# Masking the decays on GpSimd, loading the weights in three groups, and a new order of the steps

## What is computed

```python
q, k = silu(conv(xn @ Wq)), silu(conv(xn @ Wk))       # 12 heads of 64, conv has 4 taps
v    = silu(conv(xn @ Wv))                            # 12 heads of 128
gk   = -exp(A_log) * softplus(xn @ Wgk + dt_bias)
beta = sigmoid(xn @ Wb + b_b)
for t in range(L):                                    # per head
    S     = S * exp(g[t])
    delta = (v[t] - k[t] @ S) * beta[t]
    S     = S + outer(k[t], delta)
    o[t]  = q[t] @ S
attn = (rmsnorm(o) * gnorm * silu(xn @ Wg)) @ Wo
h    = silu(fq(xn) @ fq(w_gate).T) * (fq(xn) @ fq(w_up).T)
out  = x + attn + fq(h) @ fq(w_down).T
```

## Time and profile before

| what | us |
|---|---|
| median of 3 runs | 3115.01 |
| lowest and highest run | 3111.84, 3118.43 |
| profiled execution, its own time | 3109.63 |
| its span, first to last instruction | 3107.9 |
| mean granted PE clock, share of 2.4 GHz | 0.931 |

### The profile page before, as it was taken

One profiled execution on the slowest core, in us unless ns is written; L12 is line 12 of the kernel. 1 busy time (PEld: TensorE's weight loads), 2 busy tenths in 40 slices (PEclk: granted clock), 3 DMA queues, 4 the chain that ended last, 5 costly groups with the idle time before them and its releaser, 6 DMA issues. The chain is left out here.

```text
span 3107.9 us, 84227 instructions
## 1 busy us (share of the span) xinstructions
PE 2683.1 (86%) x25361; PEld 2160.6 (70%) x25487; DVE 2498.6 (80%) x7140; ACT 2210.9 (71%) x6626; POOL 1621.8 (52%) x2418
## 2 busy tenths in 40 slices
...
GB/s 52 32 32 15 33 34 32 28 36 16 31 36 27 34 32 17 33 35 26 35 24 24 35 26 35 36 14 33 36 25 36 25 24 34 35 26 35 25 22 22
DMA packets 319515, 92.14 MB, mean 30 GB/s; under 512 B 283056, under 2 KB 310000, under 8 KB 318960
## 3 DMA queue, kind: packets, MB, share of 16 engines
...
## 5 line engine op out<-in xcount | busy, mean ns | idle before, releaser
L611 POOL TENSOR_TENSOR laneA<-laneA,laneT 96x30 f32<-96x30 f32 (+14 forms) x960 | 518.8, 540 | 75.2
L608 POOL TENSOR_TENSOR laneT<-laneA 96x30 f32<-96x30 f32 (+14 forms) x960 | 494.5, 515 | 70.4
L911 DVE SCALAR_TENSOR_TENSOR vc<-ring,cvv,vc 128x255 f32<-128x255 f32 (+2 forms) x1152 | 463.8, 472 | 22.3 <-ACT vc L713 22.0
L911 DVE SCALAR_TENSOR_TENSOR KQ<-ring,ckq,KQ 128x255 f32<-128x255 f32 (+2 forms) x1152 | 460.0, 472 | 16.5 <-DVE nabs L943 6.5
L622 POOL TENSOR_TENSOR rO<-ov,mhalf 128x8 f32<-128x8 f32 x96 | 159.6, 1662 | 377.3 <-DVE ov L1060 371.7
L1004 DVE SCALAR_TENSOR_TENSOR UP<-ring,cj,gm 128x256 f32<-128x256 f32 x768 | 315.4, 475 | 44.6 <-PE ring L1190 39.0
L595 POOL TENSOR_TENSOR sqk<-sse,phalf 128x8 f32<-128x8 f32 x96 | 157.1, 1636 | 350.5 <-DVE sse L978 350.5
L808 ACT ACTIVATE junk<-V 128x128 f32<-128x128 f32 x768 | 230.3, 305 | 77.7 <-DVE V L1055 64.7
L1190 PE MATMUL ring<-KQ 64*128 64x256 f32 x768 | 238.2, 453 | 54.8 <-DVE KQ L911 41.3
L773 ACT ACTIVATE eps<-bank_e 128x128 f32<-128x128 f32 x384 | 105.8, 276 | 225.8 <-PE bank_e L1326 184.6
L589 POOL TENSOR_TENSOR gm<-g,mle 128x512 f32<-128x512 f32 x192 | 197.7, 1048 | 128.6 <-DVE UP L1004 72.4
...
## 6 DMA issues: line engine op xcount, KB each, us to landing
to_lanes<-UP SPq DMA_DIRECT2D x128, 96.0 KB, 2.8
...
UP<-from_lanes SPq DMA_DIRECT2D x128, 96.0 KB, 3.1
...
```

The costliest lines, as they stand in the source:

```text
L608: link(nc.gpsimd.tensor_tensor(t, A[:, 0:m, j:j + 1].broadcast_to([LANES, m, n]), A[:, j:j + 1, j + 1:BLK].broadcast_to([LANES, m, n]), AL ...
L611: link(nc.gpsimd.tensor_tensor(w, w, t, ALU.add))
L911: ins = nc.vector.scalar_tensor_tensor(acc[:, n, s:T], src[:, n * T:n * T + T - s], wt(n)[:, TAPS - 1 - s:TAPS - s], acc[:, n, s:T], ALU.m ...
```

## The change

The bf16 product of DD is gone. Instead a new step DDm multiplies the exponentials on POOL with the 0/1 mask mle, in place, and GRr waits for it (semaphore s_mask) and not for ACT. The loads are in three groups, each with its own semaphore: x of the first item and nine loads that the first projections and gates need; the value weights (two); and the late ones (eight: feed-forward, gnorm, Wo, Wg). The rounding and turning of the feed-forward weights, and wo times gnorm, move to FU 0 of the first item. LN's load of item 0 is now issued at the very start.

ORDER is new. The parts of it that are spoken of below, as they stand before and after:

- XN, XNr: first in the list for the next item; now near the end of the list before it (offset 2 in place of 1, XNr with a wait for GP 5, whose input buffer it overwrites). VT 3, VTr 3 go from the end of the list to its beginning (of the next iteration). VPs 4, VPs 5 and XR now stand at the end, where they stood behind the beginning or in the middle.
- Beginning of the list now: VT 3, ZB, QK 0, ZBr, QKr 0, VTr 3, VT 2, QK 1, QK 2, ZBe, QKt 0, ZBg, QK 3. The end: ... WO 4, WO 5, HTr 0, KTr 1, HT 1, VPs 5, LANEP 7, HTr 1, YOr.
- LN: from between VPt 0 and DD 3 to behind GRr 11.
- GRr: before, GRr 0 to 3, SE 3 to 5, GRr 4, SO 5, SE 6, GRr 5, XQ0's second half, SO 6, MX 2, SO 7, ..., GR 3, GRr 6, ... GRr 11 behind SE 9. Now GRr 0 to 3, QN 2, QN 3, DDg 5, SSr 1, all of XQ0, CJ 1, DDm 2, MX 1, DDm 3, SE 3, GRr 4, DDm 4, SE 4, GRr 5, DDm 5, QN 5, SSr 2, GR 3, GR 4, GRr 6, GRr 7, GR 5, CJ 2, GRr 8, GRr 9, SE 5, SO 5, GRr 10, GRr 11, MX 2, SE 6.
- DDm 0 stands behind VPt 2, DDm 1 behind MYr 0, both ahead of MZ 0.
- LOUT behind SE 7 (before, behind FUm 0 and ahead of SE 10); LANEP 0 and 1 ahead of OS 0, LANEP 2 and 3 behind OS 0 and OS 1, 4 to 7 behind OS 2 (before, all behind OS 0).

The diff, cut to its core:

```diff
-WEIGHTS_FROM, WEIGHTS_TO = ("ZBr", 0), ("QKt", 2)
+WEIGHTS_AT = ("FU", 0)
+NW_FIRST, NW_LATE = 9, 8
...
@@ block.sync: x, then Wk, Wq, Wgk, Wb, conv_k, conv_q, dt_bias, b_b, A_log @@
+                sp.dma_start(xin[:, :, :], x_v[0]).then_inc(s_x, 16)
                 sp.dma_start(wqk[:, 0, :], Wk).then_inc(s_wload, 16)
...
+                sp.dma_start(wv[:, :], Wv).then_inc(s_wval, 16)
+                sp.dma_start(cvv[:, :, :], conv_v.rearrange("(h c) t -> c h t", c=P)).then_inc(s_wval, 16)
...
+                sp.dma_start(wg[:, :], Wg).then_inc(s_wlate, 16)
...
@@ block.gpsimd @@
+                    if kind == "DDm":
+
+                        pool.wait_ge(read("DD", a), rv(i, "DD", a))
+                        nc.gpsimd.tensor_tensor(out=decay(a), in0=decay(a),
+                                                in1=mle[:, :].unsqueeze(1).unsqueeze(1).broadcast_to([P, 2, NT, P]),
+                                                op=ALU.mult).then_inc(s_mask, 1)
@@ block.scalar, XN (VP of the first item: wait for s_wval) @@
+                        if not early(i):
+
+                            split(act, full("XN", 0), full("GP", 5))
+                            act.wait_ge(full("GP", 5), rv(i - 2, "GP", 5))
@@ block.vector @@
-            dve.wait_ge(s_wload, 16 * 19)
             dve.wait_ge(s_setp, 3)
...
             def feed_forward_weights(link):
 
+                dve.wait_ge(s_wlate, 16 * NW_LATE)
+                nc.vector.tensor_scalar(wo[:, :, :], wo[:, :, :], gw[:, 0:1], None, ALU.mult).then_inc(s_setd, 1)
...
-                    if zero(i) and (kind, a) == WEIGHTS_FROM:
+                    if zero(i) and (kind, a) == WEIGHTS_AT:
                         feed_forward_weights(link)
-                    if zero(i) and (kind, a) == WEIGHTS_TO:
                         turned_weights(link)
...
-                        dve.wait_ge(read("DD", p), rv(i, "DD", p))
+                        dve.wait_ge(s_mask, cnt(i, NP, p + 1))
@@ block.tensor @@
-            pe.wait_ge(s_setd, 1)
+            pe.wait_ge(s_wload, 16 * NW_FIRST)
...
-                        mm(b[:, :], mgt[:, :], decay(a).rearrange("p h t n -> p (h t n)"), start=True, stop=False)
-                        mm(b[:, :], identb[:, :], negm[:, :, :].rearrange("p u n -> p (u n)"), start=False, stop=True)\
+                        mm(b[:, :], mgt[:, :], decay(a).rearrange("p h t n -> p (h t n)"), start=True, stop=True)\
                             .then_inc(full("DD", a), 1)
```

More of the change, by code:

```diff
@@ L26 @@
 KEEP = ((("ZBr", 0, 1), ("XQ0", 0, 1)), (("ZB", 0, 1), ("QK", 2, 1)), (("ZBr", 0, 1), ("QKt", 2, 1)), (("QK", 2, 1), ("FU", 0, 1)), (("GPr", 0, 0), ("OG", 0, 0)), (("GPr", 1, 0), ("OG", 1, 0)), (("GPr", 2, 0), ("OG", 2, 0)), (("GPr", 3, 0), ("OG", 3, 0)), (("GPr", 4, 0), ("OG", 4, 0)), (("GPr", 5, 0), ("OG", 5, 0)))
-WEIGHTS_FROM, WEIGHTS_TO = ("ZBr", 0), ("QKt", 2)
+WEIGHTS_AT = ("FU", 0)
+NW_FIRST, NW_LATE = 9, 8
 ORDER = (
[L53 to L66, removed]
[7 rows of a table removed]
-    ("XQr", 0, 1), ("SQ", 9, 0), ("GRr", 9, 1), ("SE", 9, 0), ("GRr", 10, 1), ("GRr", 11, 1), ("SO", 9, 0),
[8 rows of a table removed]
-    ("GP", 2, 0), ("OTr", 0, 0), ("GPr", 2, 0), ("KTr", 1, 1), ("OTr", 1, 0), ("SO", 16, 0), ("SE", 16, 0),
[5 rows of a table removed]
-    ("OG", 4, 0), ("OT", 4, 0), ("GPr", 5, 0), ("VTr", 3, 1), ("OTr", 3, 0), ("LANEP", 6, 1), ("HT", 0, 1),
-    ("OG", 5, 0), ("WO", 3, 0), ("OTr", 4, 0), ("OT", 5, 0), ("HT", 1, 1), ("OTr", 5, 0), ("WO", 4, 0),
-    ("WO", 5, 0), ("HTr", 0, 1), ("LANEP", 7, 1), ("HTr", 1, 1), ("VPt", 5, 1), ("YOr", 0, 0),
@@ new lines @@
+    ("VT", 3, 0), ("ZB", 0, 1), ("QK", 0, 1), ("ZBr", 0, 1), ("QKr", 0, 1), ("VTr", 3, 0), ("VT", 2, 0),
+    ("QK", 1, 1), ("QK", 2, 1), ("ZBe", 0, 1), ("QKt", 0, 1), ("ZBg", 0, 1), ("QK", 3, 1), ("QKr", 1, 1),
+    ("QKt", 1, 1), ("VP", 0, 1), ("GC", 0, 1), ("DDg", 0, 1), ("VT", 5, 0), ("STORE", 0, 0), ("QKr", 2, 1),
+    ("QKt", 2, 1), ("QKr", 3, 1), ("VPr", 0, 1), ("TSTORE", 0, 0), ("VTr", 2, 0), ("TFETCH", 0, 0),
+    ("GCr", 0, 1), ("VTr", 5, 0), ("QKt", 3, 1), ("VP", 1, 1), ("QKs", 0, 1), ("QKs", 1, 1), ("QKs", 2, 1),
@@ new lines @@
+    ("VPr", 1, 1), ("VT", 4, 0), ("QK", 4, 1), ("DD", 0, 1), ("VTr", 4, 0), ("VPt", 1, 1), ("DDg", 1, 1),
+    ("DD", 1, 1), ("VP", 2, 1), ("QT", 0, 1), ("QKs", 3, 1), ("QKr", 4, 1), ("DDg", 2, 1), ("DDr", 0, 1),
+    ("QKt", 4, 1), ("VPr", 2, 1), ("FETCH", 0, 0), ("DD", 2, 1), ("DDr", 1, 1), ("QT", 1, 1), ("DDr", 2, 1),
+    ("QTr", 0, 1), ("VPt", 2, 1), ("DDm", 0, 1), ("MY", 0, 0), ("MY", 1, 0), ("MYr", 0, 0), ("DDm", 1, 1),
+    ("QT", 2, 1), ("QTr", 1, 1), ("QTr", 2, 1), ("QT", 3, 1), ("DDg", 3, 1), ("MZ", 0, 0), ("QN", 0, 1),
@@ new lines @@
+    ("QN", 1, 1), ("VPt", 0, 1), ("QK", 5, 1), ("MZr", 0, 0), ("MYr", 1, 0), ("DD", 3, 1), ("SSr", 0, 1),
+    ("MY2", 0, 0), ("QKr", 5, 1), ("DDr", 3, 1), ("QTr", 3, 1), ("CJ", 0, 1), ("MY2r", 0, 0), ("QKs", 4, 1),
+    ("QKt", 5, 1), ("GR", 0, 1), ("GRr", 0, 1), ("GRr", 1, 1), ("GR", 1, 1), ("QKs", 5, 1), ("GRr", 2, 1),
[4 rows of a table added]
+    ("DDm", 4, 1), ("SE", 4, 0), ("DDr", 5, 1), ("QTr", 5, 1), ("MZ", 2, 0), ("GRr", 5, 1), ("DDm", 5, 1),
+    ("QN", 5, 1), ("SSr", 2, 1), ("MZr", 2, 0), ("GR", 3, 1), ("GR", 4, 1), ("VPs", 0, 1), ("GRr", 6, 1),
[3 rows of a table added]
```

55 lines of the change are left out of this document (34 added, 21 removed), and 37 rows, old and new, of the table ORDER.

## The result

| | runs, us | profiled execution, us |
|---|---|---|
| kernel before | 3117.64 (3111.84 to 3123.48, 5 runs) | 3109.63 |
| changed kernel | 3095.24 (3092.36 to 3100.74, 5 runs) | 3095.24 |

The ratio is 0.9932, 95% interval 0.9914 to 0.995: faster by 0.7%. The forecast was 3092. The number came out 3 us off, but three of its terms were far off, and they cancelled. The page first: the busy line, then three of its groups (line, engine, operation, count, busy us, mean ns of one, idle time before it and what ended it).

A forecast was written before the change was run, and what follows sets the result against it. No engine bounds it everywhere: DVE the first stage, PE the last, the middle shared. 3109.6 - 19.5 (start) - 6 (turns) + 3 (iterations) = 3087, so 3092 for the runs' median; range 3045 to 3150.

The forecast's parts named there:

- The stages and the walk: One iteration: SO 5 comes later, PE's work and waits behind it shrink; +0.1 us with contention, bounds -1.5 and +2.5.
- rival A: PE's last stage: its waits go too, 1.5 us an iteration less, 3045; chance 0.12.
- Contention: XQ0 and CJ 1 on DVE beside POOL's DDg and DDm: one more wait, 0.6 us an iteration, at most 2.5.
- DDm 2 hidden with 2 us to spare: POOL ahead of GRr 4: some 4.2 us to DDm 2's end, covered by over 6 us of DVE work.
- The removed product: DD's bf16 product on PE: removal worth 0 to 1.3 us an iteration, nothing booked for it separately.
- The turns: 12 loop turns: with XN done before the turn, 0.5 us less each, 6 in all.
- The 5.5 stays: Loop turns: PE's 5.5 us idle while the branch is taken and code comes was to remain.
- The start: First iteration: split loads and postponed weights bring the next iteration 10.3 us earlier and remove a 9.2 wait, 19.5 together.
- no 9 us gap ahead of DD 0: After the first iteration: PE's 9.17 us wait for DDg behind the lane solve goes, since the solve ends early enough.
- rival D: Start: quantising the weights isn't hidden, 3103; chance 0.08.
- B: SO 5 too late: PE runs dry for GRr 4 to 9, perhaps half clock; +1.7 us an iteration, 3140; chance 0.35.
- C: POOL late: lane solve ends 1 us after PE asks for DD 0, each iteration 1 us longer, 3122; chance 0.05.

The follow-up runs named there:

- e1: Changed kernel with the mask back on PE (bf16 product in DD, no DDm on POOL), new order and weight groups kept: 2983.29 us, ratio to before 0.9581.
- e8: Changed kernel with both halves of XQ0 moved to the end of the iteration before, behind YOr, mask still on POOL: 3076.31 us.
- e12: As e9, but DDm 4 waits for GRr 4 on DVE and not for XQ0's end: 2982.39 us, ratio to before 0.9584.
- e3: Changed kernel with both halves of XQ0 moved in the order to behind GRr 11, nothing else: 3093.63 us.
- e9: Changed kernel with DDm 2 to 5 spread away from XQ0, DDm 4 and 5 waiting for XQ0's end: 3008.26 us.
- e5: Kernel before with the mask alone changed (DDm on POOL, DD one product), old order and old start: 3084.83 us.
- e2: Changed kernel with DDm cut from 512 columns to 16, order, waits and weight groups kept: 2972.39 us.
- e10: Kernel before with six more PSUM-clearing products at the start, 12 PE instructions ahead of the loop: 3057.87 us.
- e6: Kernel before with XN and XNr alone moved into the iteration before: 3055.59 us.
- e4: Changed kernel with the old start (one group of 19 loads, feed-forward weights quantised ahead of the first ZBr): 3109.71 us.

## Why the prediction was right in its number, point by point

- **The stages and the walk.** I forecast SO 5 4.6 us later in the iteration and the stretch behind it 5.1 shorter (3.5 of PE's work and 1.6 of waits), -0.5 together without contention. With SO 5 from its first instruction and the iteration from the end of YOr's copy, e1 has it 5.5 later and the rest 6.5 shorter (39.9 and 49.8 us before, 45.4 and 43.3 in e1). The walk was right to 1 us. By mean periods it is -1.55 a plain iteration. Small as that looks, the difference to my -0.5 stands for 30 iterations, 31 us of the sum, and it is the size that rival A gave to the last stage's waits.
- **Contention, the term that failed.** I took 0.6 us an iteration, one more wait of the kind of L839, with 2.5 as the upper bound, since POOL would also wait for CJ's power between DDm. It did so only once, between DDg 5 and DDm 2: DDr 2 to 5 came in time, so DDm 2 to 5 ran back to back and met four instructions of XQ0. That is 3.8 us of DVE and 3.6 of the period, beyond my bound, and 112 us in all (e1, e8, e12). I had counted conflicts, and should have laid POOL's queue beside DVE's.
- **The size of a DDm.** I used DDg's 1.05 for it. Undisturbed (e3, e9) it is 1.27, and 1.34 beside XQ0. Its first input is read in full where DDg's repeats one value, and it writes in place; which of the two makes the difference no run separates. That is +42 us of POOL on top of 201, hidden in itself, but it lengthens each conflict.
- **The rule of the Trainium skill** (SBUF — State Buffer, "Who interferes with whom") that I weighed as a danger held in the rows shown here. DVE instructions with two SBUF inputs, and a tensor_scalar of f32, wait for a whole POOL instruction (1.25 to 1.38); the taps (0.47), GRr (0.87 a pair), which have one input in PSUM, and the tensor_reduce of QN (0.68) keep their time. (One exception the other way: in e5 a tensor_scalar of two columns, `veps<-mv`, met DDm 13 times and kept its 0.17.) It did not hold for POOL's power: the product of L860, two SBUF inputs, began in its midst and took 0.42. There the measurement decides. I had the rule and the list of candidates, and booked one sixth.
- **DDm 2 hidden with 2 us to spare.** It was, behind XQ0; e3, which takes XQ0 away, shows the price without that cover: 2.35 us.
- **The removed product.** DD to DD is now 0.86 (two of them take 1.88, the last of which 1.02), as forecast. With the mask nearly free (e2 against e1) it is worth 0.3 us an iteration, from a range of 0 to 1.3.
- **The turns, the second failed term.** "The 5.5 stays", and 6 us for XN. It fell to 2.4 (29.2 us over 12, by PE's waits), and turns gained 5.4 each over plain iterations, 65 us in all. Measured in the same way, as what a turn adds to a plain period (8.45 before, 4.73 in e10, 3.53 in e6, 3.06 now), a shift of the code is worth 45 us (before to e10), XN's move another 14 (e10 to e6), and 6 are not separated. I took a wait named "issue" for one wait; it was two.
- **The start.** 19.5 forecast; in e4 18.7 at the first copy, and 14.5 to 18 in the time. From the kernel before to the changed one the first copy gains only 9.0, as with the old start (e4) the changed kernel reaches it 9.6 later than the kernel before: 6.6 of that is contention in the first two iterations (e1), the rest isn't separated. The steps:

```profile
13.99 2.43 DVE L926 SCALAR_TENSOR_TENSOR KQ<-ring,ckq,KQ 128x255 f32<-128x255 f32 x6 [1.43 <-ACT KQ L707]
...
61.10 2.12 SPq L497 DMA_DIRECT2D to_lanes<-UP  x4
...
64.71 1.01 DVE L879 TENSOR_SCALAR wo<-wo,gw 128x1536 f32<-128x1536 f32 x1
...
84.81 0.28 DVE L899 COPY wd<-bank_e 96x128 f32<-96x128 f32 x1
...
108.40 1.92 POOL L628 COPY laneX<-laneA 72x1024 f32<-72x1024 f32 x1 [0.18 <-POOL laneA L622]
108.91 0.21 DVE L958 TENSOR_TENSOR z<-ring,zbias 128x48 f32<-128x48 f32 x1 [1.42 <-PE ring L1169]
```

Taps at 14.0 for 15, LOUT at 61.1 for 60, the solve's end at 108.4 for 104, no 9 us gap ahead of DD 0 (in e4 it is 10.22). But the next iteration's ZBr stood at 108.9: the weights took DVE 20.4 us with the waits for their transposition, not 16.4, and the work behind them 23.8, not 18. In e4 this ZBr stands at 116.25, so the new start is worth 7.3 us there, where I had 10.3; the 3 missing are rival D in a milder form.

- **The rivals.** B had the mechanism: PE runs dry for GRr and then goes at half the clock. It forecast +1.7 an iteration, and the plain ones became 2.05 longer, but ahead of GR 3 and not of SE 6. It did not decide, because the turns gave back what it took. There is a touch of C: PE waits for POOL's DDg once an iteration, 0.4 us each (12.1 over 32), not 1. Had the code of the kernel before begun 12 instructions further on, as in e10, the changed kernel as it is would measure 37 us slower than it and not 22 faster.

So the terms were -19.5, -6 and +3; by periods they are -9, and of the iterations 12 x -5.4 = -65 for the turns and 30 x 2.05 = +62 for contention less the order's gain (-2 is left for the last iteration). With e1 between them, the forecast's -19.5 for the start, -15 for the order, -6 for the turns and +18 for contention stand against -16, -46, -62 and +112. The order and the turns gave 87 us more than forecast, the mask took 94 more. The sum was right by luck.
